# A five-stage transformer block on one core: one program block with hand-overs by semaphore, a later transposition of half of the maxima, and a second set of banks for the last scores

## The reference

```python
h = concatenate([edges(x), txt], axis=1)             # 8 x 384 x 256
h = h + attn0(layernorm(h))    # 16 heads of 16, two softmaxes (keys K and K'), mixed by alpha
h = h + ffn0(layernorm(h))     # fp4 quantise x and weights, silu(gate) * up, quantise, down; 704 wide
h = h + anchors(layernorm(h))  # 16 heads of 64, 64 anchors: softmax over anchors, sums, products
h = h + experts(layernorm(h))  # shared GEGLU (1024 wide) + one of 8 experts chosen by argmax
```

## Time and profile before

| | us |
|---|---|
| median of 3 runs | 1839.74 (1838.70 to 1842.72) |
| the profiled execution | 1838.02 |
| its span, first to last instruction | 1836.2 |
| PE busy | 1754.4 (96%) |
| DVE busy | 1005.3 (55%) |
| ACT busy | 678.0 (37%) |
| POOL busy | 409.4 (22%) |
| mean granted TensorE clock | 0.985 of full speed |

### The profile page before, as it was taken

How to read it: one execution, slowest core, us unless ns; L and a number is a source line. 1 busy time by engine, 2 the same in 40 slices (tenths; PEclk the granted TensorE clock), 3 DMA queues, 4 the chain that set the end, 5 groups by cost and what they waited for, 6 DMA issues and landing times. The chain is left out here.

```text
span 1836.2 us, 29116 instructions
## 1 busy us (share of the span) xinstructions
PE 1754.4 (96%) x9935; PEld 1119.1 (61%) x9935; DVE 1005.3 (55%) x2073; ACT 678.0 (37%) x1290; POOL 409.4 (22%) x415
## 2 busy tenths in 40 slices
PE   7989999899999998999999999999999999999997
PEld 3324444444444434677756566566767669999997
DVE  6597877778778886788874544443211211222221
ACT  2106656566566676445533232233111110111110
POOL 2101021120211012888831222110221211000000
PEclk9989999999999999999999999999999999999999
DMA  6733532425424302000065000000000003432311
GB/s 194 130 65 66 92 79 40 91 56 92 79 41 90 77 2 73 1 0 0 1 238 160 1 0 0 0 1 1 26 35 17 34 20 109 146 129 101 106 31 34
DMA packets 111955, 112.84 MB, mean 61 GB/s; under 512 B 11455, under 2 KB 104433, under 8 KB 111858
## 3 DMA queue, kind: packets, MB, share of 16 engines
q1 hardware_dynamic: 98610, 83.21, 20.1%
q10 hardware_dynamic: 9600, 18.92, 2.9%
q0 software_dynamic: 3648, 9.46, 1.4%
HBM read 78.51 MB, written 32.93 MB: 61 GB/s over the span
## 5 line engine op out<-in xcount | busy, mean ns | idle before, releaser
L949 DVE TENSOR_REDUCE mx<-ps_a 128x1 f32<-128x384 f32 x768 | 380.4, 550 | 55.2 <-PE ps_a L579 53.2
L808 ACT ACTIVATE prob<-ps_a 128x768 f32<-128x768 f32 (+1 forms) x512 | 306.2, 650 | 104.3 <-PE ps_a L592 102.8
L579 PE MATMUL ps_a<-w,qs 96*128 96x384 bf16 x768 | 244.3, 338 | 10.3 <-DVE mx L949 5.5
L592 PE MATMUL ps_a<-qs,w 100*128 100x384 bf16 x768 | 208.4, 331 | 6.3 <-issue 3.7
L2181 PEld LDWEIGHTS ps_e<-xTr,w 128*128 128x128 f32 x1792 | 206.1, 193 | 2.2 <-issue 0.8
L2181 PE MATMUL ps_e<-xTr,w 128*128 128x128 f32 x1792 | 206.4, 277 | 0.6 <-DVE xTr L2354 0.6
L579 PEld LDWEIGHTS ps_a<-w,qs 96*128 96x128 bf16 x768 | 74.8, 98 | 188.3 <-DVE mx L949 102.9
L603 PE MATMUL ps_a<-prob,vp 128*32 128x384 f32 x1536 | 163.3, 498 | 0.0
L2118 PE MATMUL ps_e<-xT_all,w 128*128 x448 | 145.7, 486 | 0.0
L2244 ACT ACTIVATE gel_r<-ps_e 128x512 f32<-128x512 f32 x56 | 33.4, 597 | 280.9 <-PE ps_e L2181 280.9
L1630 PE MATMUL ps_m<-w 128*128 128x352 f32 x384 | 124.8, 470 | 4.5 <-ACTq L1853 3.1
(11 more groups left out here) (266 smaller groups left out, 2587.1 us busy)
## 6 DMA issues: line engine op xcount, KB each, us to landing
w<-parts_dram SPq DMA_DIRECT2D x192, 96.0 KB, 5.3
w<-in_L_ffn_W_dram ACTq DMA_DIRECT2D x18, 1024.0 KB, 8.3
parts_dram<-w SPq DMA_DIRECT2D x24, 576.0 KB, 3.4
qs<-parts_dram SPq DMA_DIRECT2D x96, 96.0 KB, 4.0
prob<-in_x_dram SPq DMA_DIRECT2D x24, 256.0 KB, 3.6
w<-in_L_ffn_W_dram SPq DMA_DIRECT2D x6, 1024.0 KB, 12.7
grouped_x<-empty_row SPq DMA_DIRECT2D x1, 4352.0 KB, 24.1
grouped_h<-empty_row SPq DMA_DIRECT2D x1, 4240.5 KB, 32.6
```

What stands on the lines that cost most here:

```text
L579: mm = pe.matmul(ps[:, r % 3, 0:T], qs[0:NS, b, u // 2, t * P:(t + 1) * P], ks[0:NS, b, u % 2, u // 2], start=True, stop=True)
L592: mm = pe.matmul(ps[:, 4 + t, 0:T], ks[0:NS + 4, b, kp, hh, t * P:(t + 1) * P], qs[0:NS + 4, b, hh], start=True, stop=True)
L808: act.activation(prob[:, g % 2, j, ts.start:ts.stop], ps[:, 4 + ts.start:4 + ts.stop, 0:T], ACT.Exp).then_inc(exp_done.sem, 1)
L949: dve.tensor_reduce(at, ps[:, r % 3, 0:T], AX.X, ALU.max).then_inc(ring_free.sem, 1)
```

## The change

Four things are changed.

1. All three stages are written into one `Block`. The barriers and clearings between the stages go. Each stage returns a dictionary of semaphores, and the next one's engines wait for single entries of it (`wait_for`). The semaphores of `attention0` are cleared by POOL inside `middle`, after its last work for the anchor attention; the engines wait for that (`freed`) where `experts` begins. The other two stages' semaphores are cleared together at the end. Some pairs of semaphores are merged.
2. In `RING` the first transposition comes three products later (`LAG = 3`), and waits as a product does. The last entry (the second transposition) has unit 31 to itself; the other 97 entries are spread over 31 units. `mx` now has a plane for each half.
3. In the last image the scores go to banks 4 to 6 in even units and to banks 0 to 2 in odd ones. Of the 21 statistics, 18 move into the turn of image 6.
4. In the first image of the feed-forward the scaling of tile (1, 0) comes before the first hidden part, on DVE, ACT and POOL.

The diff without the change of indentation, cut:

```diff
 def end_stage(nc, G):
-    nc.clear_and_free_semaphores(G["semaphores"])
-    nc.all_engine_barrier()
-    G["semaphores"] = []
+    ended, G["semaphores"] = G["semaphores"], []
+    return ended
...
+def wait_for(eng, done, *names):
+    for name in names:
+        signal, i, n = done[name]
+        eng.wait_ge(signal.sem, signal.at(i, n))
...
-    RING = [(u, t) for u in range(HALF) for t in range(TT)] + [(0, None)] \
-        + [(u, t) for u in range(HALF, UNITS) for t in range(TT)] + [(1, None)]
+    LAG = 3
+    RING = [(u, t) for u in range(UNITS) for t in range(TT)]
+    RING.insert(NM + LAG, (0, None))
+    RING.append((1, None))
...
-        return range(NR * v // UNITS, NR * (v + 1) // UNITS)
+        last = UNITS - 1
+        return range((NR - 1) * v // last, (NR - 1) * (v + 1) // last) if v < last else range(NR - 1, NR)
...
+    def scores_at(v, more):
+        return 4 if more or v % 2 == 0 else 0
...  # PE, ring
-                        back = 3 if t is not None else 1
+                    back = 1 if r == NR - 1 else LAG
...  # PE, scores
-                    pe.wait_ge(exp_done.sem, exp_done.at(i, max(2 * v + part - 1, 0)))
+                pe.wait_ge(exp_done.sem, exp_done.at(i, max(2 * v + part - (1 if more else 3), 0)))
+                if v == 1 and not more:
+                    pe.wait_ge(ring_free.sem, ring_free.at(i + 1, 0))
...  # DVE, turn
+                    if more and not more2 and 24 <= v < 30:
+                        gather_moments(v - 24, v - 23)
                         if v == UNITS - 8 and not more:
-                            gather_moments(0, B - 1)
+                        gather_moments(B - 2, B - 1)
...  # middle: SP, DVE, POOL, PE, ACT
+            wait_for(sp, done0, "values", "output")
...
                 inputs(0, 2)                      # DVE, and POOL alike
+            inputs(1, 0)
...
+            pool.wait_ge(h1_done.sem, h1_done.at(B - 1, 0))
+            pool.wait_ge(gs_done.sem, gs_done.at(B - 1, 0))
+            pool.wait_ge(g_done.sem, g_done.at(B - 1, 0))
+            pool.wait_ge(bo_in.sem, 16)
+            nc.clear_and_free_semaphores(ended)
+            pool.sem_inc(freed.sem, 1)
...
+            wait_for(pe, done0, "first", "added")
...                                               # ACT, turn of the first image
-                        if early:
-                            size_inputs(*tile_at(i, t, 2))
+                    if first and t == 0:
+                        size_inputs(*tile_at(i, t, 3))
...
-                size_inputs(0, 2)
+            wait_for(act, done0, "moments")
...  # experts
+    def enter(eng):
+        wait_for(eng, done1, "freed")
+        eng.sem_inc(done1["entered"][0].sem, 1)
...
+            enter(pe)
+            wait_for(pe, done1, "inputs", "weights")
                 for a in range(IT1):
+                if a == 1:
+                    wait_for(pe, done1, "sums")
                     gate_up(0, a)
...
+            enter(act)
+            wait_for(act, done1, "moments")
...
+        with nc.Block() as block:
+            done0 = attention0(nc, block, G, E, ...)
+            ended = end_stage(nc, G)
+            done1 = middle(nc, block, G, ..., done0, ended)
+            ended = end_stage(nc, G)
+            experts(nc, block, G, E, W1, W2, W3, Wg, out, done1)
+        nc.clear_and_free_semaphores(ended + end_stage(nc, G))
+        nc.all_engine_barrier()
```

More of the change, by code:

```diff
@@ L1190, in _ @@
[L1190 to L1197 removed]
+            inverses(2, 2, B)
+            for_images(dve, turn)
+            normalize(B - 1, GROUPS - 2)
+            normalize(B - 1, GROUPS - 1)
+            dve.memset(F.hz[:, :, INTER0:], 0.0).then_inc(w4_zero.sem, 1)
@@ new lines, in _ @@
+            for t in range(FIRST_TILES):
+                quantize_first(t)
+            add(B - 1, 0)
+            new_moments(B - 1, range(2))
+            add(B - 1, 1, 7)
+            new_moments(B - 1, range(2, TT))
+            gather_moments(B - 1, B)
+            dve.wait_ge(hm_done.sem, hm_done.at(B, 0))
+        return {"moments": (hm_done, B, 0), "added": (h_done, B, 0), "output": (op_done, B, 0), "values": (av_done, B, 0),
+                "first": (w4_copied, 0, len(moves) // 4 + 1)}
@@ L1206, with middle @@
 TINY = 1.1754943508222875e-38
-def middle(nc, G, wemb, wanc, wout, bout, E, w1s, w2s, w3s, W1, W2, W3):
+def middle(nc, block, G, wemb, wanc, wout, bout, E, w1s, w2s, w3s, W1, W2, W3, done0, ended):
     h, mv, rstd, ident, bn = G["h"], G["mv"], G["rstd"], G["ident"], G["bn"]
@@ L1929 @@
+        return {"freed": (freed, 0, 1), "entered": (entered, 0, 0), "sums": (h1_done, B, 0), "moments": (aggr_done, 0, NT - KNOWN),
+                "outputs": (out_done, B, 0), "inputs": (entry_xT, 0, 1), "weights": (expert_w_in, 0, 16 * 9),
+                "empty": (empty_in, 0, 32)}
 E8 = 8
@@ L1952, in expert_buffers, with experts @@
             "hs": nc.dram_tensor("grouped_h", [(SLOTS1 + 1) * P, C + 1], F32, kind="Internal").ap()}
-def experts(nc, G, E, W1, W2, W3, Wg, out):
+def experts(nc, block, G, E, W1, W2, W3, Wg, out, done1):
     h, mv, rstd, ident = G["h"], G["mv"], G["rstd"], G["ident"]
@@ new lines, in _ @@
+        @block.sync
+        def _(sp):
+            enter(sp)
+            sp.wait_ge(wg_zero.sem, 1)
+            sp.dma_start(wg[:, :, 0:E8], Wg.rearrange("(k p) e -> p k e", p=P)).then_inc(wg_in.sem, 16)
+            sp.wait_ge(x_placed.sem, 16 * NT)
+            sp.dma_start(xg[:], xs_dram[0:P]).then_inc(x_in.sem, 16)
+            sp.wait_ge(rt_done.sem, 1)
+            sp.dma_start(xg[:], xs_dram[P:2 * P]).then_inc(x_in.sem, 16)
+            for b in range(2):
+                sp.wait_ge(h_placed[b].sem, h_placed[b].at(B // 2, 0))
+            sp.dma_start(hp[:], hs_dram[0:P]).then_inc(hp_in.sem, 16)
+            total = sp.value_load(start_i[0:1, E8:E8 + 1], min_val=0, max_val=SLOTS1)
+            with sp.Fori(0, total) as s:
+                wait_all(sp, (rt_done, s, 2))
+                sp.dma_start(xg[:], xs_dram[bass.ds((s + 2) * P, P)]).then_inc(x_in.sem, 16)
+                wait_all(sp, (id_done, s, 1))
+                sp.dma_start(hp[:], hs_dram[bass.ds((s + 1) * P, P)]).then_inc(hp_in.sem, 16)
+            wait_all(sp, (x_in, total, 32), (hp_in, total, 16), (y_out, total, 0))
+            sp.sem_inc(all_out.sem, 1)
+            sp.wait_ge(all_out.sem, 1)
```

3015 lines of the change are left out of this document (1486 added, 1529 removed).

## The result

The changed kernel takes 1818.53 us (median of 4 runs, 1816.67 to 1821.30) beside 1839.22 us for the kernel before, a ratio of 0.9885 with a 95% interval of 0.9866 to 0.9904: 21 us faster. The forecast was 1813.6, with 1804 to 1826 as the range. The profiled execution took 1817.46 us; its span, first to last instruction, is 1815.7.

A forecast was written before the change was run, and what follows sets the result against it. PE was taken as the bound, busy 96% of the span. Terms 4.8 + 3.3 + 3.8 - 0.3 + 5.1 + 4.9 + 4.8 - 0.3 = 26.1 us off 1838.0 gave 1811.9, plus 1.7 for the median: 1813.6, range 1804 to 1826.

The forecast's parts named there:

- Part 2, the transpositions: Attention turns: PE's 0.69 us mid-turn wait goes in seven turns, 4.8 us; shorter waits at five borders give 3.3.
- The moved statistics: Turn 6 of the attention: taking over 18 statistics from the last image costs 0 to 1.3 us, 0.3 taken.
- Part 3, the last image: Last attention image: two sets of banks and fewer statistics on DVE give 3.8 us, bounds 1.3 to 8.0.
- once they are early, DVE alone sets the end: Last attention image: with ACT's exponentials early, DVE, busy 45.69 of 50 us, sets the end; its gain is 3.8.
- Rival (b): Last attention image: DVE is not the bound, ACT's pace is reached, 8.0 us instead of 3.8; 1809.4, chance 0.08.
- a last image of over 48 us: Sign against the prediction: it is wrong if the last attention image still takes over 48 us.
- Parts 1 and 4, the first hand-over and the first image: Attention to feed-forward: earlier start 2.6 and clock 2.5 us; earlier scaling of tile (1, 0) 4.9; 10.0 stay.
- From 748.20 on PE is full, so these 10.0 us stay: Feed-forward behind its first image: PE fills the stretch, so the 10.0 us saved in front stay saved.
- Part 1, the second hand-over: Anchor products to experts: 3.4 us of gap and 1.8 of clock, less 0.4 waiting for image 1's inputs: 4.8.
- Rival (a): Borders and feed-forward's first image: other waits close up, the clock falls again; gain only 15.6 us, 1824.1, chance 0.18.
- (c): Both hand-overs give nothing since engines must fetch the next stage's code; 5.1 and 4.8 go, 1823.5, chance 0.06.
- (d): Feed-forward and anchor loops: new code layout makes 7 back edges miss at 5.7 us each, 1853.6, chance 0.05.

The follow-up runs named there:

- experiment 1: The changed kernel with the old order of the transpositions alone (RING, ring_part and back as before): 1825.73 us, ratio to the kernel before 0.9921.
- experiment 6: The changed kernel with ACT's exponentials of the last image for 192 of 384 columns only: last image 47.68 us, one whole run 1804.84 us.
- experiment 7: The changed kernel with PE's scores and values of the last image for 256 of 384 columns only: last image 47.08 us, one whole run 1806.90 us.
- experiment 11: The changed kernel with five small moves against remaining waits, among them later turned outputs, the second transposition and DVE's later addition: 1816.67 us, ratio 0.9870.
- experiment 12: The changed kernel with four moves: silu first on ACT, later turned outputs, first feed-forward tile in bank 3, experts' second gate products earlier: 1815.12 us, ratio 0.9869.
- experiment 10: The changed kernel with ACT's silu and copy of turned inputs ahead of the next inputs' squares in the feed-forward: 1818.74 us, ratio 0.9885.

## Why the prediction was right, and where its terms were off

**Part 2, the transpositions: right, 7.7 for 7.8.** The sum hides two errors that cancel, so its closeness is partly luck: a full turn gained 1.6 us where I had 1.34 (more of the border's 1.5 went than I took; the wait that is left is 0.63 and not 0.8), while turns 0 and 3 gained less, 0.35 (with the 1.1 of the mark taken off) and 0.32, where I had 1.34 and 0.69. These two turns do not repeat well: in the kernels with the new order turn 0 takes 70.31 to 70.96 us and turn 3, which holds the back edge, 78.75 to 79.63. The moved statistics cost 0.24 in turn 6 (65.26 in experiment 1 against 65.02), for which I had 0.3.

**Part 3, the last image: the step that failed.** It said of the exponentials that "once they are early, DVE alone sets the end". They did not get early enough. DVE's half of the sum held: where PE or ACT is relieved (experiments 6, 7, 11 and 12) DVE has its last normalisation done 47.0 to 47.6 us after the mark, against 50.07 before, or 51.2 counted from the new mark; that is 3.6 to 4.2 less, for 3.8 forecast. But in the changed kernel PE gets there last. Its work of 1.38 us a unit (0.59 for scores, 0.79 for values) fills the unit, with ACT 2% behind, and it still waits six times 0.2 us and once 0.80 for ACT's copies. The row was there: PE was busy 47.05 of 50 us, more than DVE's 45.69. I had put the 0.21 of ACT down to the bank alone, while PE had work of 1.38 for a unit of 1.40; in the new profile ACT still waits 0.18 a unit, which I had said would go. So the gain was 2.8 and not 3.8. Rival (b), 8.0, was never to be had: it asks for some 43 us from the new mark, and PE is busy for 45.80. The prediction named a last image of over 48 us as a sign of being wrong. It takes 48.45 from the mark where it now stands and 47.28 from the old one, so the sign was set on a mark that moved and decides nothing.

**Parts 1 and 4, the first hand-over and the first image: right, 10.2 for 10.0.** The gap gave 2.4 (2.6 forecast), the clock 2.9 (2.5), and the order of the first image 4.9 (4.9). The clock gave more than the first eight products, since the next stretch of the kernel before was still partly at the low level; the same work now takes 2.68 us at 1.00:

```profile
722.97:726.14 3.17, 3.17 (x10) 2.02 (x10) 1.68 (x6) 0.46 (x1) 0.13 (x1) 0.82 1.10 357
```

The new wait in front of `down` is 1.76 (1.6), for the reason given: ACT's `copy_hidden` behind the squares.

**"From 748.20 on PE is full, so these 10.0 us stay": wrong by 1.1.** PE was full there because it was late. DVE, POOL and ACT need 8.31 us for a tile, PE 8.20. In the kernel before, PE had lost 4.18 us to POOL, the side engines had a lead, and PE went twelve tiles at 8.20 to 8.30 before it stood 0.33 us in every image (8.20, 8.20 and 8.53 us a tile, 8.31 in the mean). In the changed kernel that begins with the fourth tile. Part of a wait that is removed in front of a stretch comes back in it, when its side engines are slower than its bound.

In the side engines' round one product on DVE stands out. That the 8.31 come from it is argued and not shown: no run took its delay away for good.

```profile
726.05 0.42 DVE L1373 SCALAR_TENSOR_TENSOR w<-w 128x256 f32<-128x256 f32 x1
...
759.60 1.68 POOL L1577 TENSOR_TENSOR w<-w 128x704 f32<-128x704 f32 x1 [0.46 <-ACT w L1853]
759.65 1.92 DVE L1373 SCALAR_TENSOR_TENSOR w<-w 128x256 f32<-128x256 f32 x1
```

Alone it takes 0.42 us; begun 0.05 us behind a product of POOL it takes 1.92 and ends 0.29 behind it. The Trainium skill, "SBUF — State Buffer", section SBUF: two separate sides, says that the port pair which both engines share is an exclusive lock, held for a whole instruction, and that a DVE operation with two SBUF inputs is blocked by a GpSimd operation that reads SBUF and began first. The rows agree with it: DVE's product ends only after POOL's. In the other direction they agree in the main: where DVE is first (751.84 in experiment 10), POOL takes 1.86 instead of 1.67, but DVE's own 0.59 instead of 0.42 is more than that rule asks for.

**Part 1, the second hand-over: 4.3 for 4.8.** The wait for image 1's inputs is 0.80 and not 0.35. DVE's last statistic ends 1.79 us behind the last anchor product as before; from there I had taken one microsecond for `inputs(1)`, and it is 0.47 of idle time and 1.06 of work:

```profile
1241.11 0.31 DVE L1559 BATCH_NORM_AGGREGATE mv<-bn 128x2 f32<-128x6 f32 x3
...
1241.89 1.06 DVE L2293 TENSOR_SCALAR xall<-h,mv,rstd 128x256 f32<-128x256 f32 x3 [0.47 <-DVE mv L1559]
```

**Rivals (a), (c) and (d).** Rival (a) put most of its loss at the borders and in the feed-forward's first image, where the sum held and the clock did not fall. (Its 2.5 for part 2 is not that part's lower bound, which by the two ranges given is -1; nothing hangs on it.) Rivals (c) and (d) had no part. Between the stages PE has no "issue" wait; the one at the back edge stays, 4.03 for 3.66. The Trainium skill ("Runtime: NRT & Kernel Launch", Instruction fetch mechanics) has it that fetching in sequence is mostly hidden and that a taken branch out of the two-page window stalls the engine. The rows agree at both places; where the pages lie no run shows. The clearing at the end can't be told apart: the experts and the end take between 570.93 and 571.99 us in the eight profiled kernels whose experts are the changed kernel's and choose the same.

**The preparation** took 2.8 us more in the changed kernel's profile. Its order of work is the same but for the place of one transposition. In the 14 profiled executions of this study it ends between 134.96 (the kernel before, and the twelfth kernel) and 142.26 us; what makes it vary stays open. So the difference of two profiles is not one of the kernels here. Whether the kernel before is quicker there on average stays open; that the medians differ by 21 and the other stretches by 23 us could mean that.

Of the 4.9 us between forecast and median, then, 1.1 are the side engines' pace, 1.0 the last image, 0.5 the second hand-over and 0.4 the end, and the first hand-over gave 0.2 more than forecast; the other 2.1 are the preparation and the scatter of whole runs, which this study can't part.

## What to carry to other kernels

Before a wait's price is booked as a gain, compare the period of each engine in the stretch behind it with the bound's: side engines that are 0.11 us a tile slower turn part of it back. When two engines are both over 90% busy in a stretch, cut the work of one at a time; the one whose cut moves nothing is hidden, whatever its share says. Then read whose wait comes last in the other cuts: the hidden engine can be the one that stops the next gain. Before comparing a stretch between two kernels, make sure that its landmark has not moved within its own period. And a barrier costs more than its gap if it lets TensorE's clock fall: here 2.4 us and 2.9 behind it, and 3.4 us and 1.8.

## What the runs showed of the hardware

A DVE product of 256 columns takes 0.42 us alone and 1.92 beside a POOL product of 704 that began 0.05 us earlier; DVE's products that read a bank of PSUM (`L1395`, 0.51 to 0.52) are not stretched beside POOL's. Eight gate products take 2.60 us after 0.74 us of idle PE and 5.04 after 4.53. Idle times of PE that differ by a few tenths (1.88 and 2.01 us, with what stood before them) went with a clock that held in one version and fell in the next; the twelve `down` instructions behind them took 2.86 us in the one and 4.54 in the other. The "issue" wait at the back edge of the attention loop took 2.58 to 4.16 us in 14 profiles.
